# A float32 attention block: each key chunk's weighted sum issued in two halves of 256 queries, and a shorter loop on ScalarE

## The reference, cut to what matters

```python
Q = (x @ Wq.T + bq).reshape(b, t, HQ, HD).transpose(0, 2, 1, 3)   # b 4, t 1024, HQ 32, HD 16
K, V = ...                                                        # 8 key/value heads
Q, K = _rope(Q, K)
K = jnp.repeat(K, G, axis=1); V = jnp.repeat(V, G, axis=1)        # G = 4 query heads share one
scores = jnp.einsum('bhqd,bhkd->bhqk', Q, K) / np.sqrt(HD)
w = jax.nn.softmax(scores, axis=-1)
attn = jnp.einsum('bhqk,bhkd->bhqd', w, V)
```

## Time and profile before

| | |
|---|---|
| median of three runs | 3173.89 us |
| profiled execution, own time | 3172.22 us |
| its span (first to last instruction) | 3170.4 us |
| TensorE busy | 3010.3 us, 95% |
| VectorE busy | 1925.7 us, 61% |
| ScalarE busy | 1685.0 us, 53% |
| attention, start of the first and of the last exponential | 1043.2 and 2321.6 us |

### The profile page before, as it was taken

The page is one execution under the profiler, slowest core; times in us unless marked ns, Lnnn a source line. Parts: engine busy times, 40 slices in busy tenths (PEclk is TensorE's granted clock), DMA queues, the critical chain, the costliest instruction groups (busy, mean ns, idle before and its releaser), DMA issues. The chain is left out here.

```text
span 3170.4 us, 52638 instructions
## 1 busy us (share of the span) xinstructions
PE 3010.3 (95%) x16201; PEld 1149.3 (36%) x16214; DVE 1925.7 (61%) x2349; ACT 1685.0 (53%) x3156; POOL 752.2 (24%) x644
## 2 busy tenths in 40 slices
PE   7889999999997999999999999999989899999999
PEld 4444444444663222222222222222233444444444
DVE  7952222222777999999999999999822322222221
ACT  5733333332111788888888888888820333333332
POOL 0144444444442000000000000000013344444444
PEclk9999999999997899999999999999999999999999
DMA  4301111001332011111111111111237111111000
GB/s 129 125 30 41 40 41 40 34 19 52 97 104 69 22 30 30 29 29 30 30 29 29 28 29 29 30 30 29 83 125 249 40 41 41 40 40 40 31 18 31
DMA packets 163964, 161.01 MB, mean 51 GB/s; under 512 B 62552, under 2 KB 100824, under 8 KB 163808
## 3 DMA queue, kind: packets, MB, share of 16 engines
q1 hardware_dynamic: 163808, 159.30, 16.5%
HBM read 111.48 MB, written 47.19 MB: 50 GB/s over the span
## 5 line engine op out<-in xcount | busy, mean ns | idle before, releaser
L1742 DVE TENSOR_REDUCE at_neg_max<-at_max_ps 128x1 f32<-128x1024 f32 x1024 | 1207.5, 1220 | 40.5 <-PE at_max_ps L1628 22.4
L1730 ACT ACTIVATE at_probs<-at_score_ps 128x512 f32<-128x512 f32 x2048 | 1057.7, 605 | 186.0 <-PE at_score_ps L1648 178.2
L1628 PE MATMUL at_max_ps<-at_km,at_q 48*128 48x512 f16 x2048 | 706.5, 394 | 13.8 <-PEq L1221 8.1
L1648 PE MATMUL at_score_ps<-at_q,at_ks 50*128 50x512 f16 x2048 | 626.5, 385 | 56.9 <-ACT at_probs L1730 41.8
L1655 PE MATMUL at_out_ps<-at_probs,at_v 128*32 128x512 f32 x4096 | 549.5, 609 | 0.1
L1648 PEld LDWEIGHTS at_score_ps<-at_q,at_ks 50*128 50x128 f16 x2048 | 153.5, 94 | 667.8 <-ACT at_probs L1730 553.2
L977 DVE SCALAR_TENSOR_TENSOR f_h<-f_up_ps,hr_factor,f_gate 128x512 f32<-128x512 f32 x128 | 96.1, 751 | 477.1 <-ACT f_gate L1051 475.0
L1924 POOL TENSOR_TENSOR rows<-rows,bias 128x512 f32<-128x512 f32 x32 | 39.4, 1265 | 1421.8 <-ACTq L1863 1334.9
L407 DVE SCALAR_TENSOR_TENSOR f_h<-f_up_ps,hr_factor,f_gate 128x512 f32<-128x512 f32 x112 | 83.9, 750 | 394.8 <-PE f_up_ps L746 241.0
L1051 ACT ACTIVATE f_gate<-f_gate_ps 128x512 f32<-128x512 f32 x128 | 76.4, 597 | 353.6 <-PE f_up_ps L1124 353.6
L1073 POOL TENSOR_TENSOR f_h_lo<-f_h,f_h_hi 128x512 f16<-128x512 f32 x128 | 148.3, 1158 | 379.3 <-ACT f_h_hi L1040 379.3
(11 more groups left out here) (145 smaller groups left out, 3642.5 us busy)
## 6 DMA issues: line engine op xcount, KB each, us to landing
rows<-x SPq DMA_DIRECT2D x40, 1024.0 KB, 5.7
x<-rows SPq DMA_DIRECT2D x16, 1024.0 KB, 4.4
f_raw<-units SPq DMA_DIRECT2D x48, 256.0 KB, 2.6
at_q<-qk_parts SPq DMA_DIRECT2D x384, 32.0 KB, 1.7
rows<-x SPq DMA_DIRECT2D x32, 256.0 KB, 2.7
at_q<-at_max_parts SPq DMA_DIRECT2D x512, 1.0 KB
att<-at_out SPq DMA_DIRECT2D x256, 32.0 KB
ao_a<-att SPq DMA_DIRECT2D x8, 1024.0 KB
```

The lines of the kernel that those rows point to most:

```text
L1628: done = nc.tensor.matmul(max_ps[u % 2][:, half * QB:(half + 1) * QB], q[k][rows, j // SLOTS, h * QB + c * P:h * QB + (c + 1) * P], km[k][ ...
L1648: nc.tensor.matmul(score_ps[pos % RING][:], ks[k][rows, kc * P:(kc + 1) * P], q[k][rows, j // SLOTS, h * QB:(h + 1) * QB], start=True, sto ...
L1730: nc.scalar.activation(probs[:, kc % PBUF, j, :], score_ps[pos % RING][:], ACT.Exp, scale=HD ** -0.5).then_inc(exps, 1)
L1742: nc.vector.tensor_reduce(neg_max[:, h, column:column + 1], max_ps[u % 2][:], AX.X, ALU.max, negate=True).then_inc(maxed, 1)
```

## The change

`weigh` gets a fourth argument, `part`. Part 0 multiplies the first 256 queries of the four heads and part 1 the last 256; the same four weight tiles are used in both. Part 0 is issued behind the second score (and its maxima half) and part 1 behind the fourth. The wait for the probabilities stands at part 0 and the completion is signalled after part 1. On ScalarE the loop over two groups at a time becomes one group written out and then a loop over the remaining 31 groups, one at a time.

```diff
-            def weigh(n, k, kc):
-                pe.wait_ge(exps, n * SU + ((kc + 1) * GH + RING))
+            def weigh(n, k, kc, part):
+                if part == 0:
+                    pe.wait_ge(exps, n * SU + ((kc + 1) * GH + RING))
+                cols = slice(part * (QB // 2), (part + 1) * (QB // 2))
                 for j in range(GH):
-                    last = nc.tensor.matmul(out_ps[2 * HD * j:2 * HD * (j + 1), :], v[k][:, kc, :],
-                                            probs[:, kc % PBUF, j, :], start=(kc == 0), stop=(kc == KC - 1),
+                    last = nc.tensor.matmul(out_ps[2 * HD * j:2 * HD * (j + 1), cols], v[k][:, kc, :],
+                                            probs[:, kc % PBUF, j, cols],
+                                            start=(kc == 0 and part == 0), stop=(kc == KC - 1 and part == 1),
                                             tile_position=(0, 2 * HD * j))
-                last.then_inc(pv_done, 1)
+                if part == 1:
+                    last.then_inc(pv_done, 1)
...
                             if follow >= 1:
                                 maxima(n + NB, 1 - k, h, kc * MSTEP + i // 2, i % 2)
-                        if kc == 0 and not first:
-                            weigh(n - 1, k if h else 1 - k, KC - 1)
-                        elif kc >= 1:
-                            if kc == 1:
-                                pe.wait_ge(out_copied, n + 1)
-                            weigh(n, k, kc - 1)
+                            if i % 2 == 0:
+                                continue
+                            if kc == 0 and not first:
+                                weigh(n - 1, k if h else 1 - k, KC - 1, i // 2)
+                            elif kc >= 1:
+                                if kc == 1 and i == 1:
+                                    pe.wait_ge(out_copied, n + 1)
+                                weigh(n, k, kc - 1, i // 2)
...
-            groups(act, run)
+            run(0, 0, 0, 2)
+            with act.Fori(1, NG) as G:
+                run(G, 0, 0, 2)
             copy_output(NG * NB - 1, 1, (NG - 1) * (GH * 32) + 1)
```

More of the change, by code:

```diff
@@ L1692, in run @@
                                 maxima(n + NB, 1 - k, h, kc * MSTEP + i // 2, i % 2)
-                        if kc == 0 and not first:
-                            weigh(n - 1, k if h else 1 - k, KC - 1)
-                        elif kc >= 1:
-                            if kc == 1:
-                                pe.wait_ge(out_copied, n + 1)
-                            weigh(n, k, kc - 1)
+                            if i % 2 == 0:
[6 more added lines that the diff above has]
+                                weigh(n, k, kc - 1, i // 2)
             groups(pe, run)
-            weigh(NG * NB - 1, 1, KC - 1)
+            for part in range(2):
+                weigh(NG * NB - 1, 1, KC - 1, part)
         @block.scalar
```

## The result

The changed kernel took 3192.08 us (median of five runs, 3187.95 to 3200.51) against 3174.37 us before: ratio 1.0059, 95% interval 1.0043 to 1.0075. It is slower by 0.6%, where I had forecast 1.8% faster. The profiled execution took 3200.51 us, its span is 3198.7, 28.3 more than before.

A forecast was written before the change was run, and what follows sets the result against it. A closed ring of scores, exponential and weighted sum, 2.40 us a chunk, was taken as the bound. Gains of 46 + 3.6 + 2.0 + 3.3, in all 55 us, off 3172.2 gave 3117.2, 3119 as median; forecast 3118, range 3098 to 3146.

The forecast's parts named there:

- ScalarE's loop: ScalarE's stops at its two-group loop's ends and four stray ones, 23.0 us, go; nothing added for 30 new ends.
- Rival 4: TensorE becomes the bound with weight loads laid bare, a half costing 0.83 us: slower, 3248 us; chance 0.05.
- the sum: Whole execution: 55 us gained, 46 in the loop of 56 blocks and 3.6, 2.0, 3.3 outside it.
- The weighted sum in halves: On TensorE: a half takes 0.56 us, 0.66 with the way in; chunk floor rises from 2.02 to 2.24.
- rival 1: On TensorE a half costs more, 0.69 to 0.74 us, as with a full drain at layout switches: 3138 us; chance 0.15.
- The ring and VectorE: The attention chunk's closed 2.40 us ring of scores, exponential and weighted sum opens; VectorE then bounds at 2.30, 18.93 a block.
- rival 3: ScalarE's stall does not depend on body length: 30 loop ends instead of 13, each 1.36 us, 3159 us; chance 0.07.
- SyncE's queue: Last score to landing of the next block's small DMAs takes 20.0 us, holding every second block to 19.17 us.
- Rival 2: SyncE's queue bounds harder: small DMAs land 0.5 us later, 28 blocks 0.5 longer, 3132 us; chance 0.06.

The follow-up runs named there:

- kernel with one whole chunk: The changed kernel with the weighted sum issued in each block's second chunk left whole, TensorE's loop body 1690 recorded instructions: 3210.15 us, ratio 1.0112.
- shifted twin: 127 more wait instructions ahead of TensorE's attention work, against the kernel whose second chunk's sum is whole, same 1690-instruction body: 3117.79 us, ratio 0.9822.

## Why the prediction was wrong

**The step that failed** is the last one on ScalarE's loop: "TensorE's loop still ends every four blocks ... 0.4 × 13 = 5 us are added." It measured 7.9 × 13 = 103 us, and where the body stays loaded it is nothing (0.88 from score to score across the branch). I had read ScalarE's stop at its branch correctly as a fetch, and beside it let TensorE off with the remark that it has room for 2048 instructions. The change made TensorE's body half as long again, 1246 to 1754, and with that the branch went from 0.21 and hidden to 3.3 to 4.0 us. The profile before could have warned: the 1.4 us of ScalarE showed that a loop body can be so long that its end becomes dear, and the longest TensorE loops whose ends were seen to be free had 1683 instructions, fewer than the 1754 to come. No rival had it either. Rival 4 had the right sign with the wrong mechanism; a half costs 0.57 + 0.10, and 0.56 + 0.10 were forecast.

Without that step the sum was pessimistic. 1158.0 − 103 = 1055 us is what the 56 blocks would take, where I had 56 × 19.05 = 1067 and 5 for the loop's ends. With 13.3 instead of 8.9 outside the loop the profiled execution would have come out near 3200.5 − 103 = 3097, not 3117. That the forecast missed by no more than 74 us (3192 against 3118), with 5 us where 103 came, is partly luck: two errors the other way made up for some of it.

**The weighted sum in halves**: right. Way in 0.10, half 0.57 against 0.56; TensorE's floor is 2.20 where VectorE holds nothing back, against 2.24. The drain between layouts that the Trainium skill states (TensorEngine Tiling, Key Properties; rival 1) does not show beyond these 0.1.

**The ring and VectorE**: right. VectorE is what is left, at 18.60 us a block against 18.93, and a chunk is 2.26 against 2.30. The difference is its spacing: I took 1.15 from two rounded starts, while 16 reductions and the split in 18.60 allow (18.60 − 0.53) / 16 = 1.13 at most.

**ScalarE's loop**: right, 22.7 us against 23.0, and rival 3 is out. Two things are open: the 2.9 us outside the loop were not foreseen and no run explains them, and the reading by blocks of 256 instructions does not come out of the trace. On TensorE's queue the packets are 16 KB, the block of the Trainium skill; on q14, ScalarE's, they are 8 KB. That a body of 151 is short enough is shown, where the limit lies is not.

**SyncE's queue**: right in kind and in the changed kernel also in size (19.26 against 19.17). Too rigid: one block's 20.0 us was taken for all, and with TensorE's stops removed the queue cost 60 us (3142.89 against 3083.38), where the prediction's numbers give 28 × (19.17 − 18.93) = 7. Rival 2 had 14 more, with a chance of 0.06.

**What the fetch is.** Shown: the stop comes with refetches of the whole body in every pass, and without them it is gone. In the loop's stretch of the kernel with one whole chunk q8 moves 113 packets of 16 KB and in its shifted twin 6; from one branch to the next it is nine packets, 144 KB, in the changed kernel too. Between branches they arrive without a stop; what is waited for is the first two behind the branch. The Trainium skill (Runtime: NRT & Kernel Launch, Instruction fetch mechanics) gives TensorE 128 KiB in blocks of 16 KiB, 2048 instructions. The trace agrees with the block size, and not with the reading that I made of the total: 1690 and 1754 are well under 2048. An estimate with the 256 instructions that the Trainium skill gives to a block there: 1690 instructions are 6.6 blocks, so they lie on seven or on eight depending on where they begin, and eight with one fetched ahead past the branch would make the nine packets. That would fit that seven stay and eight don't. This last step is inferred from one shift; where the blocks begin was not measured.

**What the lower clock costs.** No run separates it, but the rows allow an estimate. In the kernel with TensorE written out the clock is the lower one for 54.6 us in all within the 56 blocks' stretch, and the 11 blocks in which that falls lose 17.7 us, 0.32 us for each of the 54.6. In the changed kernel it is the lower one for 6.8 to 13.7 us behind every stop, 10.0 on average. That gives about 3.2 of the 7.9 us; 3.5 are the stop, and some 1.2 are left for the second wait.

## What to carry to other kernels

Before lengthening the code in a loop, count what it adds to each engine's loop body and look at what the loops of that length cost at their ends in the profile at hand; an engine whose loop end is free today has a limit too, and here a body of 1690 instructions was over it in one place and under it 127 instructions further on. "issue" ahead of an engine right behind a branch, together with instruction packets that grow with the number of passes, is the sign of it here. And when a stop is removed, take the spread of what is next in line from many of its occurrences, not from one.

## What the runs showed of the hardware that I had not expected

- Two matmul groups of 256 columns one behind the other take what one of 512 takes (1.01 us for 16 instructions against 1.00 for 8).
- 127 instructions that do nothing, ahead of a loop, made the kernel 92 us faster (3210 to 3118).
- With a stop of some 3.5 us at each loop end TensorE's granted clock fell from 2.4 to 1.2 GHz for 6.8 to 13.7 us in each pass, and the mean over the loop fell from 0.99 to 0.94.
- Straight code costs no stop: with TensorE's groups all written out, 81 packets of 16 KB came in during the loop's stretch (1132 to 2190 us), and no "issue" wait was over 0.8 us.
- The instruction packets are 16 KB on the queue that follows TensorE's loop (q8) and 8 KB on the one that follows ScalarE's (q14).
